# Value sums emptied on ScalarE instead of VectorE, and turned by plain transposes, in a perceiver layer

## The chip, the cores and the metric

The kernel runs on one core of a Trainium2 chip. The metric is the device time of one execution in microseconds (us): the median of several runs. TensorE multiplies matrices and writes to PSUM; VectorE and ScalarE work on rows of PSUM and SBUF; GpSimd works on SBUF alone; SyncE (SP) issues the DMAs. Each engine works through its own queue in order, and the queues wait for each other by semaphores. In the profile PE is TensorE, PEld its weight loads, DVE is VectorE, ACT ScalarE and POOL GpSimd.

## The reference

A layer of three residual blocks on 128 batches of 32 rows of 128 features: cross-attention on a context of 257 rows, causal self-attention, and a mixture of experts. The change lies in the first block alone:

```python
def _L0_xattn_ref(queries, keys, values, mask):   # keys = values = ctx
    ...
    scale = 1.0 / jnp.sqrt(jnp.asarray(E, q.dtype))
    scores = jnp.einsum('blhe,bshe->bhls', q, k)   # 16 heads of 8 features
    A = jax.nn.softmax(scale * scores, axis=-1)
    A = A * mask                                   # 32 x 257
    out = jnp.einsum('bhls,bshd->blhd', A, v)
    out = jnp.transpose(out, (0, 2, 1, 3)).reshape(B, L, -1)
    return out
...
x = x + _L0_xattn_ref(_layernorm(x, axis=-1), ctx_1024, ctx_1024, fside_SxS2_0)
```

## The kernel before, in words

Three stages run one after the other, one for each block of the reference. The first works on 16 tiles of 8 batches. A tile has 16 steps, and 8 steps (4 batches) are a half-tile; there are 32 half-tiles, counted by `m`. A step takes half of a batch's 16 heads: two groups of four heads by 32 query rows, 128 rows of scores by 257 columns of the context each.

The order is written out by hand in a `steps` function for each engine, and the engines run it with lags. In step `s` TensorE issues the `scores` of step `s`, the transposes of the probabilities of step `s - 2` (`turn_probs`), and at some steps more: at the fourth and eighth step of a half-tile the products of probabilities and values of two batches (`weigh_values`, into the PSUM tile `AV`), at the third and the seventh the transposes of context rows into keys (`turn_keys`), at the sixth `turn_out`. VectorE takes the `maxima` of step `s` and moves the turned, masked probabilities of step `s - 2` to SBUF (`keep_probs`). ScalarE does the `exponentials` of step `s` behind these maxima, and copies keys and queries.

The context has 257 rows; 256 go through TensorE and the last is added by itself. `AV` holds, for each batch, 128 rows (four groups of 32 features) by four heads and 32 queries; only where a row's head is the column's head is the value of use. In the fifth step of the next half-tile VectorE evicts `AV` to `O_m` and multiplies by that mask (`keep_sums`). In the sixth TensorE multiplies `O_m` with a 0/1 matrix `gather_d`, which turns it and adds up the four heads' columns of which three are zero (`turn_out`), into the PSUM tile `MISC`; VectorE scales it by the inverse sums of exponentials (`own_outputs`, into `O_n`). GpSimd forms the last context row's share (`last_products`) and adds it (`add_last`). Once per tile VectorE turns `O_n` (`turn_tile`) and GpSimd adds it to the residual `X` (`add_tile`). `MISC` is shared: keys, queries and outputs all go through it, so `turn_keys` waits for `own_outputs` of the half-tile before.

SP's queue is in order too. In the first tile it waits for `o_last`, which `last_products` sets, then loads the last context rows anew and issues the second half of the residual loads, and only behind them the next inputs:

```python
                    sp.wait_ge(o_last, 2 * t + 1)
                    sp.nop(nofuse=True)
                    load_all(sp, t + 1, 0)
                    if fresh:
                        for q in range(HQ // 2, HQ):
                            load_residual(q)
```

Of the kernel before, what the change touches and what calls it, by code (L numbers as in the profile page):

```python
# [9 lines left out]
ALU = mybir.AluOpType  # L10
ACT = mybir.ActivationFunctionType
# [3 lines left out]
B, L, D = 128, 32, 128  # L15
# [14 lines left out]
HSTEPS = STEPS // 2  # L30
DECAY = -0.25
# [3 lines left out]
def perceiver_layer(nc, x, ctx, fmask, Wq, bq, Wk, bk, Wv, bv, Wo, bo, gate_w, w1, b1, w2, b2, ln_g, ln_b, out):  # L35
    with ExitStack() as es:
        def sb(name, shape, dt=F32):
            return es.enter_context(nc.sbuf_tensor(name, shape, dt))
# [8 lines left out]
        gather_d = sb("gather_d", [P, NQ, DK])  # L47
# [56 lines left out]
        with ExitStack() as s1:  # L104
            def sb1(name, shape, dt=F32):
                return s1.enter_context(nc.sbuf_tensor(name, shape, dt))
# [4 lines left out]
            def sem1(name):  # L111
                return s1.enter_context(nc.semaphore(name))
# [4 lines left out]
            last_p = sb1("last_p", [P, HB * NQ])  # L117
            last_x = sb1("last_x", [P, HB * NQ, HQ, DK])
            last_y = sb1("last_y", [P, HB * NQ, 2, DK])
            last_v = sb1("last_v", [P, HB * NQ, DK])  # L120
            last_o = sb1("last_o", [P, HB * NQ, DK])
# [14 lines left out]
            rden = sb1("rden", [P, HB * NQ])  # L136
            Et = sb1("Et", [P, HSTEPS, 2, KT, HQ * L])
# [21 lines left out]
            p_last, v_last, o_last, o_both = sem1("p_last"), sem1("v_last"), sem1("o_last"), sem1("o_both")  # L159
            q_first = sem1("q_first")  # L160
            av_ps = sem1("av_ps")
            rden_set = sem1("rden_set")
# [114 lines left out]
            def _(pool):  # L277
# [32 lines left out]
                def last_products(t, h):  # L310

                    m = 2 * t + h
                    pool.wait_ge(all_in[h], 16 * (t + 1))
                    pool.tensor_tensor(last_x[:, :, :, :],
                                       last_all[:, h, :, :].rearrange("p j (g q d) -> p (j g) q d", g=NQ, q=HQ),
                                       block_of[:, :].unsqueeze(1).unsqueeze(3).to_broadcast([P, HB * NQ, HQ, DK]),
                                       ALU.mult).then_inc(v_last, 1)
                    pool.wait_ge(v_last, 3 * m + 1)
                    pool.tensor_tensor(last_y[:, :, :, :], last_x[:, :, 0:2, :], last_x[:, :, 2:4, :], ALU.add).then_inc(v_last, 1)
                    pool.wait_ge(v_last, 3 * m + 2)  # L320
                    pool.tensor_tensor(last_v[:, :, :], last_y[:, :, 0, :], last_y[:, :, 1, :], ALU.add).then_inc(v_last, 1)
                    pool.wait_ge(v_last, 3 * m + 3)
                    pool.wait_ge(p_last, m + 1)
                    pool.tensor_tensor(last_o[:, :, :], last_v[:, :, :],
                                       last_p[:, :].unsqueeze(2).to_broadcast([P, HB * NQ, DK]), ALU.mult).then_inc(o_last, 1)

                def add_last(t, h):

                    m, n = 2 * t + h, HB * NQ
                    pool.wait_ge(o_n, m + 1)  # L330
                    pool.wait_ge(o_last, m + 1)
                    mine = O_n[:, :, n * h:n * (h + 1)].rearrange("p d u -> p u d")
                    pool.tensor_tensor(mine, mine, last_o[:, :, :], ALU.add).then_inc(o_both, 1)
# [9 lines left out]
                def steps(t, fresh, final):  # L343
                    for h in range(2):
                        if not (final and h == 1):
                            place_queries(*((t, 1) if h == 0 else (t + 1, 0)))
                        if h == 1 and not fresh:
                            add_tile(t - 1)
                        if not final:
                            power(t + 1, h)  # L350
                        if not (fresh and h == 0):
                            last_products(*((t, 0) if h == 1 else (t - 1, 1)))
                            add_last(*((t, 0) if h == 1 else (t - 1, 1)))
# [12 lines left out]
                pool.wait_ge(dve_set, 11)  # L366
                run_tiles(steps, pool)
                last_products(T - 1, 1)
                add_last(T - 1, 1)
# [3 lines left out]
            def _(pe):  # L373
# [82 lines left out]
                def turn_out(t, h, final=False):  # L456
                    m = 2 * t + h
                    pe.wait_ge(o_m, m + 1)
                    if not final:
                        pe.wait_ge(kt_sb, 2 * m + 4)  # L460
                    for j in range(HB):
                        i = pe.matmul(MISC[:, 32 * j:32 * j + 32], O_m[:, j, :], gather_d[:, :, :].rearrange("p g d -> p (g d)"),
                                      start=True, stop=True)
                    i.then_inc(o_ps, 1)
# [43 lines left out]
                pe.wait_ge(dve_set, 11)  # L508
# [21 lines left out]
            def _(act):  # L530
# [35 lines left out]

# [7 lines left out]
                run_tiles(steps, act)  # L574

            @block.vector
            def _(dve):
# [49 lines left out]

                def last_probs(t, h):
                    m = 2 * t + h
                    dve.wait_ge(rden_set, m + 1)  # L630
                    if not (isinstance(t, int) and t == 0 and h == 0):
                        dve.wait_ge(o_last, m)
                    dve.scalar_tensor_tensor(last_p[:, :], E[:, h, :, S - 1], mask_col[:, 0:1],
                                             rden[:, :], ALU.mult, ALU.mult).then_inc(p_last, 1)

                def keep_sums(t, h):

                    m = 2 * t + h
                    dve.wait_ge(av_ps, HB * (m + 1))
                    dve.tensor_tensor(O_m[:, :, :].rearrange("p j (q l) -> p j q l", q=HQ),  # L640
                                      AV[:, :, :].rearrange("p j (q l) -> p j q l", q=HQ),
                                      hh_of[:, :].unsqueeze(1).unsqueeze(3).to_broadcast([P, HB, HQ, L]), ALU.mult).then_inc(o_m, 1)

                def own_outputs(t, h):

                    m = 2 * t + h
                    dve.wait_ge(o_ps, m + 1)
                    dve.wait_ge(rden_set, m + 1)
                    if not (isinstance(t, int) and t == 0):
                        if h == 0:  # L650
                            dve.wait_ge(o_t, t)
# [14 lines left out]
                def steps(t, fresh, final):  # L666
                    for s in range(STEPS):
# [3 lines left out]
                        if s % HSTEPS == 4 and not (fresh and s < HSTEPS):  # L671
                            keep_sums(*((t, 0) if s > HSTEPS else (t - 1, 1)))
# [9 lines left out]
                        if not (fresh and s < HSTEPS):  # L682
                            tt, ss = back(t, s, HSTEPS)
                            hh = ss // HSTEPS
                            if s % HSTEPS == 3:
                                invert(tt, hh)
                            if s % HSTEPS == 4:
# [18 lines left out]
                dve.tensor_reduce(gather_d[:, :, :], ident[:, :].rearrange("p (g q d) -> p g d q", g=NQ, q=HQ), AX.X,  # L706
                                  ALU.add).then_inc(dve_set, 1)
# [39 lines left out]
                dve.wait_ge(dve_set, 11)  # L747
# [3 lines left out]
                invert(T - 1, 1)  # L751
                last_probs(T - 1, 1)
                keep_sums(T - 1, 1)
# [952 lines left out]
```

## Time and profile before

| | us |
|---|---|
| median of 3 runs | 1048.88 (1048.84 to 1049.33) |
| the profiled execution | 1050.45 |
| its span, first to last instruction | 1048.7 |
| TensorE busy in the span | 927.9 (88%) |
| VectorE busy | 840.0 (80%) |
| ScalarE busy | 648.9 (62%) |
| GpSimd busy | 606.9 (58%) |

The first stage ends at about 529 us. A busy share over the whole span is a mean over three stages with different limits, so the rows below are from stretches of one stage. An instruction's duration reaches from its start to its end; the next one of the same engine can start before that, so what one costs in a row of them is the distance of the starts.

### The profile page before, as it was taken

What the parts mean: (1) busy time and instruction counts of PE and PEld (TensorE: products, weight loads), DVE (VectorE), ACT (ScalarE), POOL (GpSimd) and SP (SyncE); (2) the same over time, 40 slices, a digit from 0 to 9 for tenths busy, and PEclk for the clock granted to TensorE, in tenths of its full rate; (3) what the DMA queues carried; (4) which work ended last, traced back from release to release, by engine and by line L of the source; (5) the groups of instructions that cost most, each with busy time, mean ns of one, the idle gap of its engine ahead of it and who ended that gap; (6) DMA issues with size and microseconds to landing.
All of it is one profiled execution on the core that took longest, in us unless ns stands there. A gap on an engine that the chain in (4) does not pass through costs nothing. (4 is left out here: it accounts for less than half of the span.)

```text
span 1048.7 us, 25999 instructions
## 1 busy us (share of the span) xinstructions
PE 927.9 (88%) x7666; PEld 815.4 (78%) x7666; DVE 840.0 (80%) x2152; ACT 648.9 (62%) x2006; POOL 606.9 (58%) x531
## 2 busy tenths in 40 slices
PE   3959999999999999999948888878899888888983
PEld 2848888888888888888848888778788787878872
DVE  5747787878788787878758887886499999999995
ACT  2626566656666566666536666666477777767674
POOL 4335555655555564556344444443477777877786
PEclk9979999999999999999969998999999999999997
DMA  4021212212221212221400000000000000000000
GB/s 119 25 74 56 58 50 65 55 47 60 55 65 43 65 55 52 56 65 54 142 1 1 0 0 0 0 0 1 1 2 10 5 10 5 10 5 6 9 5 16
DMA packets 48676, 35.34 MB, mean 34 GB/s; under 512 B 3660, under 2 KB 48392, under 8 KB 48648
## 3 DMA queue, kind: packets, MB, share of 16 engines
q1 hardware_dynamic: 48648, 35.00, 12.2%
q8 instruction: 14, 0.23, 0.1%
q14 instruction: 14, 0.11, 0.0%
HBM read 32.88 MB, written 2.10 MB: 33 GB/s over the span
## 5 line engine op out<-in xcount | busy, mean ns | idle before, releaser
L551 ACT ACTIVATE E<-SC,neg_max 128x257 f32<-128x257 f32 x512 | 238.4, 471 | 161.2 <-DVE neg_max L613 161.1
L425 PE MATMUL SC<-Kt,Qbd 128*128 128x257 f32 x1024 | 279.6, 396 | 1.0 <-ACT E L551 0.8
L613 DVE TENSOR_REDUCE neg_max<-SC 128x2 f32<-128x514 f32 x256 | 177.0, 691 | 86.6 <-PE SC L425 75.2
L425 PEld LDWEIGHTS SC<-Kt,Qbd 128*128 128x128 f32 x1024 | 176.9, 193 | 31.4 <-issue 14.1
L301 POOL TENSOR_TENSOR Qbd<-Qt,head_scaled 128x2048 f32<-128x2048 f32 (+2 forms) x33 | 145.1, 4398 | 80.0 <-ACT Qt L541 80.0
L621 DVE TENSOR_TENSOR Et<-ETP,mask_T 128x512 f32<-128x512 f32 x256 | 174.0, 680 | 15.0 <-PE ETP L439 14.9
L439 PE MATMUL ETP<-ident,E 128*128 128x128 f32 x1024 | 156.1, 275 | 0.0
L1371 PE MATMUL PO<-W,hid 128*128 128x128 f32 x1024 | 138.2, 278 | 18.8 <-ACT hid L1412 18.7
L1371 PEld LDWEIGHTS PO<-W,hid 128*128 128x128 f32 x1024 | 131.4, 192 | 29.0 <-issue 21.5
L1436 ACT ACTIVATE Y<-Z,zb,zs 128x128 f32<-128x128 f32 x256 | 111.0, 485 | 60.1 <-DVE zb L1591 60.1
L439 PEld LDWEIGHTS ETP<-ident,E 128*128 128x128 f32 x1024 | 125.3, 142 | 20.5 <-issue 0.4
L1360 PE MATMUL PH<-xT,W 128*128 128x256 f32 x512 | 135.1, 387 | 0.5 <-ACT xT L1404 0.5
L1412 ACT ACTIVATE hid<-PH,b1c 128x256 f32<-128x256 f32 x256 | 105.5, 463 | 19.3 <-PE PH L1360 17.8
L551 ACT ACTIVATION_READ_ACCUMULATOR E<-SC,neg_max 128x1 f32 x512 | 101.1, 198 | 0.0
L308 POOL TENSOR_TENSOR xrs<-xvar,neg_half 128x1 f32<-128x1 f32 x32 | 17.6, 549 | 134.8 <-DVE xvar L593 134.8
L1360 PEld LDWEIGHTS PH<-xT,W 128*128 128x128 f32 x512 | 87.8, 192 | 9.7 <-ACT xT L1404 0.7
L1268 POOL TENSOR_TENSOR zr<-zv,neg_half 128x8 f32<-128x8 f32 x32 | 60.0, 1875 | 39.6 <-DVE zv L1577 39.6
L1262 POOL TENSOR_TENSOR XB<-xn,b2r 128x512 f32<-128x512 f32 x64 | 81.4, 1275 | 0.8 <-DVE xn L1487 0.8
L1601 DVE TENSOR_TENSOR U<-Y,gr 128x512 f32<-128x512 f32 x64 | 71.2, 1113 | 5.4 <-POOL acc L1274 2.9
L450 PE MATMUL AV<-Et,V 128*32 128x128 f32 x2048 | 69.4, 276 | 0.3 <-DVE Et L621 0.3
L1120 PE MATMUL PY<-Wo,Oc 128*128 128x128 f32 x256 | 39.1, 316 | 29.5 <-DVE Oc L887 29.5
L450 PEld LDWEIGHTS AV<-Et,V 128*32 128x32 f32 x2048 | 51.9, 109 | 11.4 <-issue 10.7
(161 smaller groups left out, 1579.1 us busy)
## 6 DMA issues: line engine op xcount, KB each, us to landing
V<-in_ctx_dram SPq DMA_DIRECT2D x64, 256.0 KB, 2.9
last_all<-in_ctx_dram SPq DMA_DIRECT2D x32, 256.0 KB, 5.0
xh<-in_x_dram SPq DMA_DIRECT2D x32, 64.0 KB, 3.7
X<-in_x_dram SPq DMA_DIRECT2D x32, 64.0 KB
out_dram<-Xo SPq DMA_DIRECT2D x64, 32.0 KB, 1.5
W<-in_L_ffn_w_dram SPq DMA_DIRECT2D x1, 1024.0 KB
W<-in_L_ffn_w_dram SPq DMA_DIRECT2D x2, 512.0 KB
last_row<-in_ctx_dram SPq DMA_DIRECT2D x32, 2.0 KB
```

The source lines that it names most:

```text
L301: pool.tensor_tensor(Qbd[:, h, j0:j1, :, :], Qt[:, j0:j1, :].unsqueeze(2).to_broadcast([P, j1 - j0, H, L]), head_scaled[:, :, :].unsqueeze ...
L425: i = pe.matmul(SC[s % 2][:, u, 0:S], Qbd[:, h, jj, g:g + HQ, :].rearrange("p q l -> p (q l)"), Kt[:, h, jj, 0:S], start=True, stop=True)
L439: i = pe.transpose(ETP[s % 2][:, c:c + P], E[:, h, u0 + u, k * P:(k + 1) * P], ident[:, :])
L450: i = pe.matmul(AV[32 * g:32 * g + 32, j % HB, :], V[:, j, k, 32 * g:32 * g + 32], Et[:, 2 * (j % HB) + g // 2, g % 2, k, :], start=(j % H ...
L551: i = act.activation(E[:, h, u0 + u, :], SC[s % 2][:, u, 0:S], ACT.Exp, bias=neg_max[:, s % 2, u:u + 1], accum_out=den[:, h, u0 + u:u0 + u ...
L613: dve.tensor_reduce(neg_max[:, s % 2, :], SC[s % 2][:, :, 0:S], AX.X, ALU.max, negate=True).then_inc(max_sb, 1)
L621: dve.tensor_tensor(Et[:, s % HSTEPS, :, :, :].rearrange("p u k c -> p (u k c)"), ETP[s % 2][:, :], mask_T[:, :, :, :].rearrange("p u k c ...
L1262: pool.tensor_tensor(XB[:, 2 * p:2 * p + 2, :, :], xn[:, :, :].unsqueeze(1).to_broadcast([P, 2, 2, D]), b2r[:, 2 * p:2 * p + 2, :].unsquee ...
L1360: i = pe.matmul(PH[x % 2][:, a, :], W1[:, x, a * P:(a + 1) * P], xT[:, :], start=True, stop=True)
L1371: i = pe.matmul(PO[p % 2][:, 2 * (x % 2) + e, :], hid[:, x % 2, a, e * P:(e + 1) * P], W2[:, x, a, :], start=(a == 0), stop=(a == FH - 1))
L1412: i = act.activation(hid[:, x % 2, a, :], PH[x % 2][:, a, :], ACT.Gelu, bias=b1c[:, FH * x + a:FH * x + a + 1])
L1436: i = act.activation(Y[:, p % 2, k, :], Z[:, p, k, :], ACT.Identity, scale=zs[:, p // 2, f:f + 1], bias=zb[:, p // 2, f:f + 1])
```

## The change

`keep_sums` moves from VectorE to ScalarE, as a plain copy without the mask, behind the exponentials of the fifth step of a half-tile (`AV_STEP = 4`). `turn_out` becomes four transposes, so `MISC` gets all four heads' columns. VectorE spreads the inverse sums over four columns of which the own one is kept (`spread_shares`, into `own_p`), and `own_outputs` multiplies all 512 columns by it (into `own_x`). The last row's share is formed the same way by one product of 512 columns on GpSimd, and `fold` adds both and then sums the four columns in two more adds. `last_products` now waits for `p_last` at its start and sets `o_last` with its one product.

```diff
+AV_STEP = 4
...
                     pool.wait_ge(all_in[h], 16 * (t + 1))
+                    pool.wait_ge(p_last, m + 1)
                     pool.tensor_tensor(last_x[:, :, :, :],
                                        last_all[:, h, :, :].rearrange("p j (g q d) -> p (j g) q d", g=NQ, q=HQ),
-                                       block_of[:, :].unsqueeze(1).unsqueeze(3).to_broadcast([P, HB * NQ, HQ, DK]),
-                                       ALU.mult).then_inc(v_last, 1)
...
-                    pool.tensor_tensor(last_o[:, :, :], last_v[:, :, :],
-                                       last_p[:, :].unsqueeze(2).to_broadcast([P, HB * NQ, DK]), ALU.mult).then_inc(o_last, 1)
...
+                                       last_p[:, :, :].unsqueeze(3).to_broadcast([P, HB * NQ, HQ, DK]),
+                                       ALU.mult).then_inc(o_last, 1)
...
+                def fold(t, h):
...
                     pool.wait_ge(o_n, m + 1)
                     pool.wait_ge(o_last, m + 1)
-                    mine = O_n[:, :, n * h:n * (h + 1)].rearrange("p d u -> p u d")
-                    pool.tensor_tensor(mine, mine, last_o[:, :, :], ALU.add).then_inc(o_both, 1)
+                    pool.tensor_tensor(last_x[:, :, :, :], last_x[:, :, :, :], own_x[:, :, :, :], ALU.add).then_inc(o_sum, 1)
+                    pool.wait_ge(o_sum, m + 1)
+                    pool.tensor_tensor(pair_x[:, :, :, :], last_x[:, :, 0:2, :], last_x[:, :, 2:4, :], ALU.add).then_inc(o_pair, 1)
...
+                    pool.tensor_tensor(O_n[:, :, n * h:n * (h + 1)].rearrange("p d u -> p u d"),
+                                       pair_x[:, :, 0, :], pair_x[:, :, 1, :], ALU.add).then_inc(o_both, 1)
...
                     for j in range(HB):
-                        i = pe.matmul(MISC[:, 32 * j:32 * j + 32], O_m[:, j, :], gather_d[:, :, :].rearrange("p g d -> p (g d)"),
-                                      start=True, stop=True)
+                        i = pe.transpose(MISC[:, j * P:(j + 1) * P], O_m[:, j, :], ident[:, :])
...
+                def keep_sums(t, h):
+
+                    m = 2 * t + h
+                    act.wait_ge(av_ps, HB * (m + 1))
+                    if not (isinstance(t, int) and t == 0 and h == 0):
+                        act.wait_ge(o_ps, m)
+                    act.activation(O_m[:, :, :], AV[:, :, :], ACT.Copy).then_inc(o_m, 1)
...
                         exponentials(t, s, first=fresh)
+                        if s % HSTEPS == AV_STEP and not (fresh and s < HSTEPS):
+                            keep_sums(*((t, 0) if s > HSTEPS else (t - 1, 1)))
...
+                def spread_shares(t, h):
+                    m = 2 * t + h
+                    dve.wait_ge(rden_set, m + 1)
+                    dve.tensor_tensor(own_p[:, :, :], rden[:, :].unsqueeze(2).to_broadcast([P, HB * NQ, HQ]),
+                                      block_of[:, :].unsqueeze(1).to_broadcast([P, HB * NQ, HQ]), ALU.mult).then_inc(own_set, 1)
...
-                    dve.tensor_tensor(O_n[:, :, HB * NQ * h:HB * NQ * (h + 1)].rearrange("p d u -> p u d"),
-                                      MISC[:, 0:P].rearrange("p (u d) -> p u d", d=DK),
-                                      rden[:, :].unsqueeze(2).to_broadcast([P, HB * NQ, DK]), ALU.mult).then_inc(o_n, 1)
+                    dve.tensor_tensor(own_x[:, :, :, :], MISC[:, :].rearrange("p (u q d) -> p u q d", q=HQ, d=DK),
+                                      own_p[:, :, :].unsqueeze(3).to_broadcast([P, HB * NQ, HQ, DK]), ALU.mult).then_inc(o_n, 1)
...
-                        if s % HSTEPS == 4 and not (fresh and s < HSTEPS):
-                            keep_sums(*((t, 0) if s > HSTEPS else (t - 1, 1)))
```

On VectorE, in the fifth and sixth step of a half-tile in the loop over tiles (`neg_max` are the maxima, `Et` the kept probabilities), there stands before:

```order
L613 TENSOR_REDUCE neg_max<-SC0 128x2 [waits exp_sb,sc_ps]
L639 ISA
L640 TENSOR_TENSOR O_m<-AV,hh_of 128x512 [waits av_ps]
L584 ISA
L586 BN_AGGR xmv<-xstat 128x2 [waits xstat_sb]
L620 REGISTER_ALU [waits et_ps]
L621 TENSOR_TENSOR Et<-ETP0,mask_T 128x512 [waits av_ps]
L593 TENSOR_SCALAR xvar<-xmv 128x1 [waits xrs_sb,xmean_sb]
L632 REGISTER_ALU [waits rden_set]
L633 SCALAR_TENSOR_TENSOR last_p<-E,mask_col,rden 128x16 [waits o_last]
L610 REGISTER_ALU
L613 TENSOR_REDUCE neg_max<-SC1 128x2 [waits exp_sb,sc_ps]
```

And now, at the same place:

```order
L622 TENSOR_REDUCE neg_max<-SC0 128x2 [waits exp_sb,sc_ps]
L593 ISA
L595 BN_AGGR xmv<-xstat 128x2 [waits xstat_sb]
L629 REGISTER_ALU [waits et_ps]
L630 TENSOR_TENSOR Et<-ETP0,mask_T 128x512 [waits av_ps]
L602 TENSOR_SCALAR xvar<-xmv 128x1 [waits xrs_sb,xmean_sb]
L647 REGISTER_ALU [waits own_set]
L648 SCALAR_TENSOR_TENSOR last_p<-E,mask_col,own_p 128x64 [waits o_sum]
L619 REGISTER_ALU
L622 TENSOR_REDUCE neg_max<-SC1 128x2 [waits exp_sb,sc_ps]
L630 TENSOR_TENSOR Et<-ETP1,mask_T 128x512 [waits av_ps,et_ps]
L658 TENSOR_TENSOR own_x<-MISC,own_p 128x512 [waits o_sum,own_set,o_ps]
```

The eviction `O_m` has left its place between the maxima of the fifth step and the variance `xvar`; the product of the own quarter, `own_x`, stands where the scaled output stood, two rows below this piece of before.

On ScalarE, in the fifth and sixth step of the loop's first half-tile (`E` are the exponentials, two of a step, and `SC0` is the score tile of the even steps), before:

```order
L551 ACTIVATE E,den<-SC0,neg_max 128x257 [waits max_sb]
L551 ACTIVATE E,den<-SC0,neg_max 128x257
L546 REGISTER_ALU
L551 ACTIVATE E,den<-SC1,neg_max 128x257 [waits max_sb]
L551 ACTIVATE E,den<-SC1,neg_max 128x257
L546 REGISTER_ALU
```

And now:

```order
L549 ACTIVATE E,den<-SC0,neg_max 128x257 [waits max_sb]
L549 ACTIVATE E,den<-SC0,neg_max 128x257
L556 ISA
L558 REGISTER_ALU [waits av_ps]
L559 ACTIVATE O_m<-AV 128x512 [waits o_ps]
L544 REGISTER_ALU
L549 ACTIVATE E,den<-SC1,neg_max 128x257 [waits max_sb]
L549 ACTIVATE E,den<-SC1,neg_max 128x257
```

The eviction stands between the exponentials of the two steps, with a wait for the value sums and one for the transposes of the half-tile before.

On TensorE, from the fifth step's score transposes to the seventh step's scores, now (before, the four rows of `O_m` were products with `gather_d` of 32 columns, at the same place):

```order
L438 MATMUL ETP1<-ident,E 128x128 [waits et_sb,exp_sb]
L438 MATMUL ETP1<-ident,E 128x128 x3
L457 ISA
L459 ISA [waits o_m]
L461 MATMUL MISC<-ident,O_m 128x128 [waits kt_sb]
L461 MATMUL MISC<-ident,O_m 128x128 x3
L421 REGISTER_ALU
L424 MATMUL SC0<-Kt,Qbd 128x257 [waits exp_sb]
L424 MATMUL SC0<-Kt,Qbd 128x257
```

The rows and waits around them are as they were: the transposes wait for `o_m`, and the scores of the next step stand behind them.

## Rows read from the trace of the kernel before

**Rows 1.** Busy time of each engine by stretches; PEclk is the granted clock.
```profile
240.00:270.00 30.00, 30.00 (x292) 25.41 (x291) 24.10 (x52) 18.47 (x69) 16.88 (x16) 1.00 0.22 57
```

**Rows 2.** Timeline of TensorE, 240 to 256 us: start, duration, instructions.
```profile
241.50 1.13 PE L425 MATMUL SC<-Kt,Qbd 128*128 128x257 f32 x4
...
242.91 1.03 PE L425 MATMUL SC<-Kt,Qbd 128*128 128x257 f32 x4
243.78 0.60 PE L439 MATMUL ETP<-ident,E 128*128 128x128 f32 x4
244.22 0.98 PE L462 MATMUL MISC<-gather_d,O_m 128*128 128x32 f32 x8
245.03 1.11 PE L425 MATMUL SC<-Kt,Qbd 128*128 128x257 f32 x4
245.98 0.60 PE L439 MATMUL ETP<-ident,E 128*128 128x128 f32 x4
246.42 0.63 PE L394 MATMUL MISC<-ident,V 128*128 128x128 f32 x4
```

**Rows 3.** Timeline of TensorE's weight loads, 243.8 to 246.9 us.
```profile
244.11 0.97 PEld L462 LDWEIGHTS MISC<-gather_d,O_m 128*128 128x128 f32 x8
```

**Rows 4.** Timeline of VectorE, 240 to 272 us; brackets are idle time before.
```profile
242.68 0.69 DVE L613 TENSOR_REDUCE neg_max<-SC 128x2 f32<-128x514 f32 x1 [0.91 <-PE SC L425]
243.29 0.68 DVE L640 TENSOR_TENSOR O_m<-AV,hh_of 128x512 f32<-128x512 f32 x1
...
245.96 0.38 DVE L652 TENSOR_TENSOR O_n<-MISC,rden 128x128 f32<-128x128 f32 x1
...
257.93 0.69 DVE L613 TENSOR_REDUCE neg_max<-SC 128x2 f32<-128x514 f32 x1 [0.91 <-PE SC L425]
...
264.48 0.43 DVE L661 STREAM_TRANSPOSE O_t<-O_n 128x256 f32<-128x256 f32 x1
```

**Rows 5.** Timeline of ScalarE, 240 to 272 us.
```profile
243.40 0.48 ACT L551 ACTIVATE E<-SC,neg_max 128x257 f32<-128x257 f32 x1 [1.49 <-DVE neg_max L613]
...
244.22 0.20 ACT L551 ACTIVATION_READ_ACCUMULATOR E<-SC,neg_max 128x1 f32 x1
...
247.73 0.20 ACT L551 ACTIVATION_READ_ACCUMULATOR E<-SC,neg_max 128x1 f32 x1
247.82 0.59 ACT L533 ACTIVATE Kt<-MISC 128x512 f32<-128x512 f32 x1
```

**Rows 6.** Groups by line and shape, 60 to 470 us: busy, mean ns.
```profile
L314 POOL TENSOR_TENSOR last_x<-last_all,block_of 128x512 f32<-128x512 f32 x26 | 27.0, 1040 | 0.0
...
L319 POOL TENSOR_TENSOR last_y<-last_x 128x256 f32<-128x256 f32 x26 | 19.1, 736 | 2.0
```

**Rows 7.** Timeline of SP's queue, 40 to 96 us.
```profile
51.85 12.57 SPq L198 DMA_DIRECT2D X<-in_x_dram  x16
...
65.95 0.38 SPq L179 DMA_DIRECT2D xh<-in_x_dram  x1
```

**Rows 8.** Timeline of GpSimd, 40 to 96 us.
```profile
48.48 1.03 POOL L314 TENSOR_TENSOR last_x<-last_all,block_of 128x512 f32<-128x512 f32 x1
...
50.95 0.41 POOL L324 TENSOR_TENSOR last_o<-last_v,last_p 128x128 f32<-128x128 f32 x1
```

**Rows 9.** Timeline of VectorE, 40 to 96 us.
```profile
72.50 0.29 DVE L580 BATCH_NORM_STATS2 xstat<-xh 128x6 f32<-128x128 f32 x1 [12.38 <-DMA xh<-in_x_dram]
```

**Rows 10.** Timeline of GpSimd, 516 to 536 us.
```profile
527.10 0.52 POOL L333 TENSOR_TENSOR O_n<-O_n,last_o 128x128 f32<-128x128 f32 x1 [2.10 <-DVE O_n L652]
```

**Rows 11.** Busy time by stretches, behind the long wait and in stage two.
```profile
74.10:80.30 6.20, 6.17 (x23) 5.51 (x24) 3.71 (x8) 2.94 (x11) 3.67 (x6) 0.50 0.04 10
...
680.00:690.00 10.00, 7.95 (x55) 7.71 (x54) 7.44 (x18) 5.63 (x15) 4.50 (x5) 0.83 0.00 0
```

**Rows 12.** Timeline of TensorE, 22 to 31 us.
```profile
27.83 1.06 PE L439 MATMUL ETP<-ident,E 128*128 128x128 f32 x4
...
29.77 0.60 PE L439 MATMUL ETP<-ident,E 128*128 128x128 f32 x4
```

More of the change, by code:

```diff
@@ L46, in perceiver_layer @@
         own_of = sb("own_of", [P, 2, HQ])
-        gather_d = sb("gather_d", [P, NQ, DK])
         hh_of = sb("hh_of", [P, HQ])
@@ L116, in perceiver_layer @@
             last_all = sb1("last_all", [P, 2, HB, D])
-            last_p = sb1("last_p", [P, HB * NQ])
+            last_p = sb1("last_p", [P, HB * NQ, HQ])
             last_x = sb1("last_x", [P, HB * NQ, HQ, DK])
-            last_y = sb1("last_y", [P, HB * NQ, 2, DK])
-            last_v = sb1("last_v", [P, HB * NQ, DK])
-            last_o = sb1("last_o", [P, HB * NQ, DK])
+            own_x = sb1("own_x", [P, HB * NQ, HQ, DK])
+            pair_x = sb1("pair_x", [P, HB * NQ, 2, DK])
             xh = sb1("xh", [P, 2, D])
@@ L136, in perceiver_layer @@
             rden = sb1("rden", [P, HB * NQ])
+            own_p = sb1("own_p", [P, HB * NQ, HQ])
             Et = sb1("Et", [P, HSTEPS, 2, KT, HQ * L])
@@ L158, in perceiver_layer @@
             et_ps, et_sb = sem1("et_ps"), sem1("et_sb")
-            p_last, v_last, o_last, o_both = sem1("p_last"), sem1("v_last"), sem1("o_last"), sem1("o_both")
+            p_last, o_last, o_sum, o_pair, o_both = (sem1(n) for n in ("p_last", "o_last", "o_sum", "o_pair", "o_both"))
             q_first = sem1("q_first")
             av_ps = sem1("av_ps")
-            rden_set = sem1("rden_set")
+            rden_set, own_set = sem1("rden_set"), sem1("own_set")
             o_m, o_ps, o_n, o_t, x1 = (sem1(n) for n in ("o_m", "o_ps", "o_n", "o_t", "x1"))
@@ L313, in last_products @@
                     pool.wait_ge(all_in[h], 16 * (t + 1))
+                    pool.wait_ge(p_last, m + 1)
                     pool.tensor_tensor(last_x[:, :, :, :],
                                        last_all[:, h, :, :].rearrange("p j (g q d) -> p (j g) q d", g=NQ, q=HQ),
-                                       block_of[:, :].unsqueeze(1).unsqueeze(3).to_broadcast([P, HB * NQ, HQ, DK]),
-                                       ALU.mult).then_inc(v_last, 1)
[L318 to L323, printed above, removed]
-                    pool.tensor_tensor(last_o[:, :, :], last_v[:, :, :],
-                                       last_p[:, :].unsqueeze(2).to_broadcast([P, HB * NQ, DK]), ALU.mult).then_inc(o_last, 1)
-                def add_last(t, h):
+                                       last_p[:, :, :].unsqueeze(3).to_broadcast([P, HB * NQ, HQ, DK]),
+                                       ALU.mult).then_inc(o_last, 1)
+                def fold(t, h):
                     m, n = 2 * t + h, HB * NQ
@@ L331, in add_last @@
                     pool.wait_ge(o_last, m + 1)
-                    mine = O_n[:, :, n * h:n * (h + 1)].rearrange("p d u -> p u d")
-                    pool.tensor_tensor(mine, mine, last_o[:, :, :], ALU.add).then_inc(o_both, 1)
+                    pool.tensor_tensor(last_x[:, :, :, :], last_x[:, :, :, :], own_x[:, :, :, :], ALU.add).then_inc(o_sum, 1)
+                    pool.wait_ge(o_sum, m + 1)
+                    pool.tensor_tensor(pair_x[:, :, :, :], last_x[:, :, 0:2, :], last_x[:, :, 2:4, :], ALU.add).then_inc(o_pair, 1)
+                    pool.wait_ge(o_pair, m + 1)
+                    if h == 0 and not (isinstance(t, int) and t == 0):
+                        pool.wait_ge(o_t, t)
+                    pool.tensor_tensor(O_n[:, :, n * h:n * (h + 1)].rearrange("p d u -> p u d"),
+                                       pair_x[:, :, 0, :], pair_x[:, :, 1, :], ALU.add).then_inc(o_both, 1)
                 def add_tile(t):
@@ L352, in steps @@
                             last_products(*((t, 0) if h == 1 else (t - 1, 1)))
-                            add_last(*((t, 0) if h == 1 else (t - 1, 1)))
+                            fold(*((t, 0) if h == 1 else (t - 1, 1)))
                 power(0, 0)
@@ L365, in _ @@
                 pool.memset(Vbd[:, :, :], 0.0).then_inc(pool_set2, 1)
-                pool.wait_ge(dve_set, 11)
+                pool.wait_ge(dve_set, 10)
                 run_tiles(steps, pool)
                 last_products(T - 1, 1)
-                add_last(T - 1, 1)
+                fold(T - 1, 1)
                 add_tile(T - 1)
@@ L507, in _ @@
                 i.then_inc(pe_set, 1)
-                pe.wait_ge(dve_set, 11)
+                pe.wait_ge(dve_set, 10)
                 turn_queries(0, 0, first=True)
@@ L574, in _ @@
                 run_tiles(steps, act)
+                keep_sums(T - 1, 1)
             @block.vector
@@ L626, in invert @@
                     dve.reciprocal(rden[:, :], den[:, h, :]).then_inc(rden_set, 1)
+                def spread_shares(t, h):
[3 more added lines that the diff above has]
+                                      block_of[:, :].unsqueeze(1).to_broadcast([P, HB * NQ, HQ]), ALU.mult).then_inc(own_set, 1)
                 def last_probs(t, h):
                     m = 2 * t + h
-                    dve.wait_ge(rden_set, m + 1)
+                    dve.wait_ge(own_set, m + 1)
                     if not (isinstance(t, int) and t == 0 and h == 0):
[L632 to L642, printed above, removed]
+                        dve.wait_ge(o_sum, m)
+                    dve.scalar_tensor_tensor(last_p[:, :, :], E[:, h, :, S - 1].unsqueeze(2).to_broadcast([P, HB * NQ, HQ]),
+                                             mask_col[:, 0:1], own_p[:, :, :], ALU.mult, ALU.mult).then_inc(p_last, 1)
                 def own_outputs(t, h):
@@ L647, in own_outputs @@
                     dve.wait_ge(o_ps, m + 1)
[L648 to L651, printed above, removed]
-                    dve.tensor_tensor(O_n[:, :, HB * NQ * h:HB * NQ * (h + 1)].rearrange("p d u -> p u d"),
-                                      MISC[:, 0:P].rearrange("p (u d) -> p u d", d=DK),
-                                      rden[:, :].unsqueeze(2).to_broadcast([P, HB * NQ, DK]), ALU.mult).then_inc(o_n, 1)
+                    dve.wait_ge(own_set, m + 1)
+                    if not (isinstance(t, int) and t == 0 and h == 0):
+                        dve.wait_ge(o_sum, m)
+                    dve.tensor_tensor(own_x[:, :, :, :], MISC[:, :].rearrange("p (u q d) -> p u q d", q=HQ, d=DK),
+                                      own_p[:, :, :].unsqueeze(3).to_broadcast([P, HB * NQ, HQ, DK]), ALU.mult).then_inc(o_n, 1)
                 def turn_tile(t):
@@ L686, in steps @@
                                 invert(tt, hh)
+                                spread_shares(tt, hh)
                             if s % HSTEPS == 4:
@@ L705, in _ @@
                                   ALU.mult).then_inc(dve_set, 1)
-                dve.tensor_reduce(gather_d[:, :, :], ident[:, :].rearrange("p (g q d) -> p g d q", g=NQ, q=HQ), AX.X,
-                                  ALU.add).then_inc(dve_set, 1)
                 dve.tensor_reduce(block_of[:, :], ident[:, :].rearrange("p (q l) -> p q l", q=HQ), AX.X,
@@ L746, in _ @@
                 dve.tensor_copy(b1c[:, :], MISC3[:, 0:NE * FH]).then_inc(dve_set3, 1)
-                dve.wait_ge(dve_set, 11)
+                dve.wait_ge(dve_set, 10)
                 run_tiles(steps, dve)
@@ L751, in _ @@
                 invert(T - 1, 1)
+                spread_shares(T - 1, 1)
                 last_probs(T - 1, 1)
-                keep_sums(T - 1, 1)
                 own_outputs(T - 1, 1)
```

## The prediction

> **What bounds the kernel now.** I read the busy table by stretches first. From 240 to 270 us, the middle of the first stage, TensorE is busy 30.00 of 30.00 us at a granted clock of 1.00; VectorE is busy for 24.10, ScalarE for 18.47, GpSimd for 16.88 [rows 1]. So TensorE sets the pace, and what a change is worth there is read from its queue alone. Next, that queue in order of time [rows 2]. A step of scores takes 0.87 us from start to start (242.91 to 243.78), four transposes of probabilities 0.44 (243.78 to 244.22), the four gather products of `turn_out` 0.81 (244.22 to 245.03), and the scores behind them 0.95 (245.03 to 245.98). No row has a wait in brackets. Then, who feeds `turn_out`: VectorE runs the maxima of step 12 (the fifth of its half) at 242.68 for 0.69 us, then at 243.29 the eviction `O_m` for 0.68, so `O_m` is there at 243.97 [rows 4]. TensorE starts loading the first `O_m` weights at 244.11, 0.14 us later [rows 3], just in time for its slot at 244.22. That eviction costs TensorE nothing today, but it has next to no margin. ScalarE does the exponentials of the same step from 243.40, behind the same maxima, and its second accumulator read starts only at 244.22 [rows 5].
>
> **What the change removes on TensorE.** `turn_out` issues 8 weight loads and 8 matmuls per half-tile (each product in two passes); it will issue 4 transposes of 128x128, the form of [rows 2] at 243.78: 0.44 instead of 0.81. The scores behind transposes take 0.87 instead of 0.95. If TensorE never waited, that is 0.37 + 0.08 = 0.45 us per half-tile.
>
> **What it adds on the path.** `keep_sums` now stands on ScalarE behind the exponentials of the step whose maxima used to stand ahead of it on VectorE. Step by step, at the same half-tile: scores start at 241.50 as before; the maxima end at 242.68 + 0.69 = 243.37; the two exponentials start at 243.40 and their last read at 244.22. The next ACTIVATE starts 0.09 us after that read's start, as 247.82 follows 247.73, so the copy starts at 244.31. The trace has no copy from `AV` on ScalarE; the nearest row is the key copy from PSUM of the same 128x512, 0.59 to 0.60 [rows 5]. `O_m` is there at 244.91, not 243.97. With the same 0.14 us the weights start at 245.05, where TensorE was ready at 244.22: a wait of 0.83. Behind the waiting transposes the next scores are queued, and everything else. Transposes 0.44 and 0.02 to fill: 245.51. Scores 0.87: the next transposes of probabilities start at 246.38, against 245.98. That is +0.40 us per half-tile. Nothing later gives it back, since TensorE has no other wait that the delay could fill, and the chain from scores over maxima and exponentials to the copy starts from TensorE itself each time. Bounds: if copy and weights lie only 0.03 apart, as the maxima's end at 243.37 and the exponentials do, it is +0.29; if the scores still take 0.95, +0.48. I take 0.40, as the 0.14 is from this very place of the loop.
>
> There are 32 half-tiles. The first lies ahead of a stall that absorbs it, the second runs at half clock right behind that stall (there the 8 passes cost twice as much, so wait and saving about cancel: +0.1), the last is the tail. 29 x 0.40 = **+11.6 us** (8.4 to 13.9).
>
> **VectorE.** It loses `O_m` (0.60 from 243.29 to the next start); `own_outputs` grows from 128x128, 0.38, to the size of the old eviction, 0.68 [rows 4]; `spread_shares` and the wider `last_p` are 64 columns, under the 0.38 of the 128-column row. They are hidden by the 0.91 idle before the maxima at 242.68. `own_x` starts when the transposes land (0.60 after the first starts, as at 243.78: about 245.7) and ends at 246.4; `turn_keys`, which waits for it, comes to its turn at 246.42 + 0.40 = 246.8, so 0.4 us of cover is left.
>
> **GpSimd.** Two 128-column products go, an add of 512 columns comes. It lies between the 512-column product (1.04) and twice the 256-column add (2 x 0.735 = 1.47) [rows 6]; I take 1.3, nearer the add. `fold` then is 1.3 + 0.74 + 0.52 and gaps of 0.1: from 246.4 to 249.2. In the other half-tile, 15.25 us later (the same maxima at 242.68 and 257.93), VectorE turns the tile at 264.48 [rows 4], now at 264.9; `fold` ends at 264.4. Hidden, with 0.5 left; without the cover it would cost a few tenths in 16 tiles.
>
> **A gain elsewhere.** At 72.50 VectorE had waited 12.38 us for `xh` [rows 9]. That load stands on SP's queue behind 16 residual loads of 12.57 us [rows 7], and these wait for `o_last`. It came with `last_o`, at 50.95 + 0.41 = 51.36; now it comes with the product, which ended at 48.48 + 1.03 = 49.51 [rows 8], and starts 0.6 earlier since the variance on VectorE no longer stands behind `O_m`. So the stall ends 2.4 us sooner: **-2.4** (0, if the loads drain no sooner, to -2.5).
>
> **The tail.** After the last half-tile nothing hides `fold`. Before, one add of 0.52 at 527.10 followed the output product [rows 10]; now 1.3 and 0.74 and their gaps come ahead of it. The shorter transposes and copy give back about what the wider `own_x` takes, and 0.15 more. **+1.9** (1.8 to 2.2).
>
> Sum: 11.6 + 0.1 - 2.4 + 1.9 = **+11.2 us** (7.8 to 16.2). The profiled execution took 1050.45 us, 1.6 above the median of the three runs; set against that median of 1048.88 it gives **1060.1**.
>
> **A rule against the change, and the clock.** A granted clock of 0.50 stood from 74.1 to 80.3 us, after VectorE's long wait had stopped TensorE; from 680 to 690, in the second stage, where TensorE is busy for 7.95 of 10 us, it is 0.83 [rows 11]: some 10 x 0.17 x 2 = 3.4 us at 1.2 GHz, which costs 1.7 us. The change puts a wait of 0.83 between two sets of transposes. Should each such place bring one such stretch, that is 1.7 us a half-tile. Against it: at 27.83 TensorE was still at 1.2 GHz (four transposes took 1.06), and having run them and one step of scores it was at 2.4 GHz by 29.77 (0.60) [rows 12]; and the middle of the first stage is granted 1.00, though ten sets of transposes at 0.44 (eight of probabilities, two of keys) take 4.4 of a half-tile's 15.25 us. The Trainium skill, "TensorE: Matmul & The Clock Gate", section on PE-mode transpose, says that transposes don't count as TensorE being busy in the same way, which speaks for the drop; the rise at 29 us speaks against it, and no row decides it for a wait of this kind.
>
> **Rivals.**
> 1. TensorE doesn't wait: the copy arrives in time, and only the saving is left. 31 x 0.45 = 14.0 off, with -2.4 and +1.9: **1034**, faster. It decides from the point where `O_m` is there 0.37 us sooner than I reckon, at 244.54. For it: the value sums are complete well before, and ScalarE idles 1.49 us ahead of these exponentials [rows 5]. Against it: ScalarE works in order, and the copy is written behind them. Chance 0.05.
> 2. The wait is about half as long (a quicker copy or restart), and saving and wait cancel: about **1049**. Chance 0.04.
> 3. The clock falls too, in half of the half-tiles: 15 x 1.7 = 26 more, **1086**; in all, about 1113. Chance 0.07.
> 4. My forecast, **1060.1**: 0.84.
>
> **How the numbers follow.** Under the forecast, the bounds give 1056.7 to 1065.1; the second stage's half-clock stretches may fall one more or one fewer, 1.7 us either way. 1055 to 1067 leaves out rivals 1 to 3, 0.16, and little else. A measurement of this kernel can tell about 0.2%, 2.1 us, from no change: faster 0.05 (rival 1), same 0.04 (rival 2), slower 0.91.
>
> **What would show it.** Right: before `turn_out`'s first transpose TensorE idles about 0.8 us for ScalarE's `O_m`, some 30 times, 24 us in all; the half-tile grows from 15.25 to about 15.65; the wait for `xh` shrinks to about 10; the add in `fold` takes 1.0 to 1.5. Wrong: no such wait (rival 1), a clock under 1.00 between 90 and 510 us (rival 3), or waits of `turn_keys` for `own_x` and of the tile's turn for `fold`, where I have cover.

## The result, and the profile after

The changed kernel took 1061.55 us (median of four runs, 1061.16 to 1062.21), the kernel before 1049.08 (four runs, 1048.84 to 1049.33). The ratio is 1.0119, with a 95% interval of 1.0102 to 1.0137: slower by 1.2%. The profiled execution took 1062.21 us with a span of 1060.5, which is 11.8 more than the span before. All that follows about the place of these 11.8 us is read from the two profiled executions.

Busy time by stretches of the changed kernel comes first, with the columns of [rows 1]: the middle of the first stage, then nearly all of that stage.

```profile
240.00:270.00 30.00, 28.66 (x277) 23.76 (x276) 23.93 (x51) 18.71 (x69) 16.93 (x14) 1.00 0.22 57
90.00:510.00 420.00, 401.84 (x3834) 334.32 (x3834) 337.65 (x687) 267.66 (x973) 243.08 (x176) 1.00 0.20 55
```

TensorE, which was busy for 30.00 of 30.00 us, now idles 1.34 us of them, and 18.16 of 420; the clock is granted in full all the way. The next view is TensorE's timeline at the place of [rows 2], with the scores behind `turn_out` of the third and of the 31st half-tile around it (these two starts measure the length of a half-tile below).

```profile
90.88 1.03 PE L424 MATMUL SC<-Kt,Qbd 128*128 128x257 f32 x4
...
243.82 1.03 PE L424 MATMUL SC<-Kt,Qbd 128*128 128x257 f32 x4
244.69 0.60 PE L438 MATMUL ETP<-ident,E 128*128 128x128 f32 x4
245.95 0.65 PE L461 MATMUL MISC<-ident,O_m 128*128 128x128 f32 x4 [0.66 <-ACT O_m L559]
246.44 1.03 PE L424 MATMUL SC<-Kt,Qbd 128*128 128x257 f32 x4
247.31 0.60 PE L438 MATMUL ETP<-ident,E 128*128 128x128 f32 x4
247.75 0.60 PE L393 MATMUL MISC<-ident,V 128*128 128x128 f32 x4
...
526.02 1.03 PE L424 MATMUL SC<-Kt,Qbd 128*128 128x257 f32 x4
```

The transposes of line 461 were due 0.44 us after 244.69, at 245.13, and start at 245.95: 0.82 late. (The bracket says 0.66 since it counts from the modelled end of the transposes ahead.) ScalarE's timeline says why:

```profile
244.31 0.48 ACT L549 ACTIVATE E<-SC,neg_max 128x257 f32<-128x257 f32 x1 [1.49 <-DVE neg_max L622]
...
245.13 0.20 ACT L549 ACTIVATION_READ_ACCUMULATOR E<-SC,neg_max 128x1 f32 x1
245.23 0.59 ACT L559 ACTIVATE O_m<-AV 128x512 f32<-128x512 f32 x1
```

The copy starts 0.10 behind the start of the second accumulator read, takes 0.59 and ends at 245.82; TensorE starts 0.13 later. ScalarE stood idle for 1.49 us just ahead of these exponentials, but the copy is queued behind them. The waits from 60 to 470 us, grouped by who waits for whom (total, times, longest):

```profile
PE MISC L461 <- ACT O_m L559: 26.3, 26, 9.6
...
DVE xstat L589 <- DMA xh<-in_x_dram: 9.5, 1, 9.5
```

Of the 26 waits the longest, 9.6, is the one in the long stall for `xh`; the other 25 share 16.7, 0.67 each. Nothing waits for GpSimd's sums here. The rows of that stall, in VectorE's timeline and then in SP's, answer to [rows 9] and [rows 7]:

```profile
70.29 0.29 DVE L589 BATCH_NORM_STATS2 xstat<-xh 128x6 f32<-128x128 f32 x1 [9.51 <-DMA xh<-in_x_dram]
```

```profile
49.17 0.37 SPq L174 DMA_DIRECT2D last_all<-in_ctx_dram  x1
49.59 12.41 SPq L198 DMA_DIRECT2D X<-in_x_dram  x16
...
63.53 0.38 SPq L179 DMA_DIRECT2D xh<-in_x_dram  x1
```

The 16 residual loads begin at 49.59 instead of 51.85, and `xh` comes to its turn at 63.53 instead of 65.95. GpSimd's timeline, in the middle of the stage and at its end:

```profile
247.41 1.27 POOL L325 TENSOR_TENSOR last_x<-last_x,own_x 128x512 f32<-128x512 f32 x1 [0.74 <-DVE own_x L658]
248.76 0.74 POOL L327 TENSOR_TENSOR pair_x<-last_x 128x256 f32<-128x256 f32 x1
249.58 0.46 POOL L331 TENSOR_TENSOR O_n<-pair_x 128x128 f32<-128x128 f32 x1
...
534.60 1.26 POOL L325 TENSOR_TENSOR last_x<-last_x,own_x 128x512 f32<-128x512 f32 x1 [0.92 <-DVE own_x L658]
535.94 0.73 POOL L327 TENSOR_TENSOR pair_x<-last_x 128x256 f32<-128x256 f32 x1
536.75 0.46 POOL L331 TENSOR_TENSOR O_n<-pair_x 128x128 f32<-128x128 f32 x1
```

The new 512-column add takes 1.26 to 1.27 us. In the tail the three adds span 534.60 to 537.21, where one of 0.52 stood [rows 10].

For the ledger two more rows of the kernel before are needed, the scores behind `turn_out` of the same two half-tiles (TensorE's timeline; `x2`, since the stretch that was asked for ends within the group of four):

```profile
93.08 0.68 PE L425 MATMUL SC<-Kt,Qbd 128*128 128x257 f32 x2
...
518.13 0.68 PE L425 MATMUL SC<-Kt,Qbd 128*128 128x257 f32 x2
```

| stretch | before | after | difference |
|---|---|---|---|
| start to the third half-tile's `turn_out` done | 93.08 | 90.88 | -2.2 |
| 28 half-tiles from there | 425.05 | 435.14 | +10.1 |
| to the first statistics of stage two (529.37, 538.96) | 11.24 | 12.94 | +1.7 |
| stages two and three, to the end of the span | 519.3 | 521.5 | +2.2 |
| sum | | | +11.8 |

A half-tile grew from 425.05 / 28 = 15.18 us to 15.54, by 0.36.

### The profile page after: what moved, and what is told of

Same layout as the page of the kernel before. It is cut to its first block and busy times, and to the rows that moved or that the text cites. A ratio compares the mean times of both kernels' runs of the same rounds, so it can differ in the third digit from the quotient of the medians.

```text
span 1060.5 us, 25732 instructions
## 1 busy us (share of the span) xinstructions
PE 917.7 (87%) x7538; PEld 800.4 (75%) x7538; DVE 849.3 (80%) x2151; ACT 664.5 (63%) x2038; POOL 619.3 (58%) x499
## 3 DMA queue, kind: packets, MB, share of 16 engines
q1 hardware_dynamic: 48648, 35.00, 11.8%
## 5 line engine op out<-in xcount | busy, mean ns | idle before, releaser
L424 PE MATMUL SC<-Kt,Qbd 128*128 128x257 f32 x1024 | 276.6, 393 | 1.0 <-ACT E L549 0.8
L1122 PE MATMUL PY<-Wo,Oc 128*128 128x128 f32 x256 | 41.7, 330 | 29.7 <-DVE Oc L889 29.7
L1122 PEld LDWEIGHTS PY<-Wo,Oc 128*128 128x128 f32 x256 | 37.8, 234 | 32.8 <-DVE Oc L889 32.8
```

The lines of the kernel that those rows point to most:

```text
L424: i = pe.matmul(SC[s % 2][:, u, 0:S], Qbd[:, h, jj, g:g + HQ, :].rearrange("p q l -> p (q l)"), Kt[:, h, jj, 0:S], start=True, stop=True)
L1122: i = pe.matmul(PY[:, e * D:(e + 1) * D], Oc[:, a:a + HQ, :, :].rearrange("p a b g -> p (a b g)"), W["o"][:, :], start=(q == 0), stop=(q = ...
```

## The experiments

The theory to test has three parts. The loss comes from where the copy stands in ScalarE's queue, not from ScalarE as such nor from the plain transposes; the transposes by themselves save about half a microsecond per half-tile; and once the wait for `O_m` is gone, `own_x` is next to be late. The rivals are that the plain turn and its wider products cost as much wherever the copy stands, that the copy moved earlier brings the whole saving and no new wait, and that the clock suffers. Each expectation gives its own numbers. Times of experiments are medians of four runs; each ratio is to seven runs of the kernel before on the same chip (1052.38 us for the first four experiments, 1051.34 for the others). The figures for a half-tile are worked out as above, over the same 28.

**The copy one step earlier.**

```diff
-AV_STEP = 4
+AV_STEP = 3
```

> The copy on ScalarE goes one step earlier, behind the exponentials of the fourth step, where ScalarE idles 1.49 us. Theory A (the wait is all in the copy's place behind the fifth step's exponentials): TensorE no longer waits for O_m and keeps its saving of 0.45 us per half-tile; but the key transposes then come to their turn before own_x is ready (own_x starts 3.89 us behind the fifth step's scores and takes 0.69, the keys are due at 4.35 to 4.46) and wait about 0.27. Net against before -0.21 per half-tile, -6 in all, with -2.4 for the earlier loads and +1.9 for the tail: 1042 us. Theory B (the wider outputs or the copy on ScalarE cost by themselves, wherever the copy stands): no change against the changed kernel, 1061. Theory C (the key transposes do not come to wait): 1036.

1042.41 us, ratio 0.9907 (0.9878 to 0.9936). No wait for `O_m` is left, and a half-tile takes 14.93. TensorE's timeline, then VectorE's:

```profile
253.18 0.60 PE L438 MATMUL ETP<-ident,E 128*128 128x128 f32 x4
253.61 0.60 PE L461 MATMUL MISC<-ident,O_m 128*128 128x128 f32 x4
254.05 1.03 PE L424 MATMUL SC<-Kt,Qbd 128*128 128x257 f32 x4
254.92 0.60 PE L438 MATMUL ETP<-ident,E 128*128 128x128 f32 x4
255.63 0.63 PE L393 MATMUL MISC<-ident,V 128*128 128x128 f32 x4
```

```profile
254.20 0.68 DVE L630 TENSOR_TENSOR Et<-ETP,mask_T 128x512 f32<-128x512 f32 x1
254.80 0.68 DVE L658 TENSOR_TENSOR own_x<-MISC,own_p 128x512 f32<-128x512 f32 x1
```

The transposes of line 461 follow those of the probabilities at once (253.18 to 253.61). The key transposes behind them don't: 0.71 here, and 0.61 to 0.62 in every other half-tile, instead of 0.44. `own_x` ends at 255.48, and TensorE goes on 0.15 later. So moving one copy by one step turns a kernel that is 1.2% slower into one that is 0.9% faster, and a second wait, which the first had covered, shows.

**The same, and `own_outputs` ahead of `keep_probs` in the sixth step.**

```diff
-AV_STEP = 4
+AV_STEP = 3
...
+                        if s % HSTEPS == 5 and not (fresh and s < HSTEPS):
+                            own_outputs(*((t, 0) if s > HSTEPS else (t - 1, 1)))
...
-                            if s % HSTEPS == 5:
-                                own_outputs(tt, hh)
```

> As the copy in the fourth step, and on VectorE own_outputs goes ahead of the sixth step's keep_probs. Theory A: own_x starts at 3.34 us behind the scores and is ready at 4.13, ahead of the keys at 4.35; no wait is left, -0.48 per half-tile against before: 1035 us. Theory B: 1061. If the probabilities kept 0.6 us later hold something up in their turn: 1042 or more.

1035.52 us (1033.93 to 1039.19), ratio 0.9841 (0.9811 to 0.9871). Its busy time by stretches, and the place in TensorE's timeline:

```profile
90.00:505.00 415.00, 414.89 (x4029) 350.48 (x4027) 349.64 (x713) 277.84 (x1019) 250.53 (x183) 1.00 0.23 64
```

```profile
250.64 0.60 PE L461 MATMUL MISC<-ident,O_m 128*128 128x128 f32 x4
251.08 1.03 PE L424 MATMUL SC<-Kt,Qbd 128*128 128x257 f32 x4
251.95 0.60 PE L438 MATMUL ETP<-ident,E 128*128 128x128 f32 x4
252.39 0.60 PE L393 MATMUL MISC<-ident,V 128*128 128x128 f32 x4
```

TensorE is again busy for all but 0.11 of 415 us, and each set of transposes here takes 0.44. A half-tile takes 14.66, 0.52 less than before. That is what the plain transposes are worth once nothing waits for them: 0.45 was reckoned, and two places that the prediction's sum left out (below) give most of the rest.

**All of the change, but the copy on VectorE at its old place.**

```diff
-                    act.activation(O_m[:, :, :], AV[:, :, :], ACT.Copy).then_inc(o_m, 1)
+                    dve.tensor_copy(O_m[:, :, :], AV[:, :, :]).then_inc(o_m, 1)
```

> All of the change but the move: the plain copy stays on VectorE at its old place behind the fifth step's maxima. Theory A: O_m is there in time, TensorE does not wait for it, but VectorE comes to own_x 0.6 us later, it ends 5.19 us behind the scores and the key transposes, due at 4.46, wait about 0.85: +0.37 per half-tile against before, 1060 us, with no wait at O_m and one of 0.8 at the keys. Theory B (the move alone is at fault, nothing else waits): 1035 to 1037.

1061.25 us, ratio 1.0093 (1.0063 to 1.0123), and 15.52 per half-tile: as slow as the change. The wait has moved. TensorE's timeline:

```profile
242.86 0.60 PE L438 MATMUL ETP<-ident,E 128*128 128x128 f32 x4
243.30 0.60 PE L461 MATMUL MISC<-ident,O_m 128*128 128x128 f32 x4
243.73 1.03 PE L424 MATMUL SC<-Kt,Qbd 128*128 128x257 f32 x4
244.60 0.60 PE L438 MATMUL ETP<-ident,E 128*128 128x128 f32 x4
245.82 0.66 PE L393 MATMUL MISC<-ident,V 128*128 128x128 f32 x4 [0.61 <-DVE own_x L655]
```

`O_m` is in time, but the key transposes, due at 245.04, start at 245.82. VectorE does the copy of 0.68 in the fifth step, runs without a gap from there, and gets to the wide `own_x` only at 245.08. So VectorE can't carry copy and wide product at these places; what ScalarE was given was work that VectorE had no room for, at a place one step too late.

**The kernel before, with only the copy moved.** The old products with `gather_d` stay; the copy goes without its mask to the place of the change, so the sums over four columns are not those of the reference.

```diff
-                    dve.tensor_tensor(O_m[:, :, :].rearrange("p j (q l) -> p j q l", q=HQ),
-                                      AV[:, :, :].rearrange("p j (q l) -> p j q l", q=HQ),
-                                      hh_of[:, :].unsqueeze(1).unsqueeze(3).to_broadcast([P, HB, HQ, L]), ALU.mult).then_inc(o_m, 1)
...
+                    act.activation(O_m[:, :, :], AV[:, :, :], ACT.Copy).then_inc(o_m, 1)
```

> The kernel before with one part alone: keep_sums on ScalarE as a plain copy behind the fifth step's exponentials, so the mask is left out and the output differs. Theory A: the wait of 0.83 us per half-tile comes in full, and the products with gather_d still take 0.81: +0.80 x 29 = 23 and 1 at the half-clock place, less about 0.6 for the earlier loads: 1072 us. Theory B (the wider outputs cost, not the place): near 1049.

1078.11 us, ratio 1.0249 (1.0221 to 1.0278): 26 slower, more than expected, and 16.07 per half-tile. TensorE's timeline:

```profile
253.28 0.60 PE L439 MATMUL ETP<-ident,E 128*128 128x128 f32 x4
254.54 1.07 PE L462 MATMUL MISC<-gather_d,O_m 128*128 128x32 f32 x8 [0.66 <-ACT O_m L561]
255.45 1.11 PE L425 MATMUL SC<-Kt,Qbd 128*128 128x257 f32 x4
```

The wait is the same, 0.82 past the due 253.72. The products then take 0.91 to the scores, where they took 0.81 without a wait [rows 2]: restarting behind a wait costs 0.10 more, which the expectation lacked. The half-tile times stand together now:

| turn | copy | us per half-tile |
|---|---|---|
| products with `gather_d` | VectorE (before) | 15.18 |
| products with `gather_d` | ScalarE, fifth step | 16.07 |
| plain transposes | ScalarE, fifth step (the change) | 15.54 |
| plain transposes | VectorE, fifth step | 15.52 |
| plain transposes | ScalarE, fourth step | 14.93 |
| plain transposes | ScalarE, fourth step, `own_x` first | 14.66 |

The move alone costs 0.89; the plain turn (with its wider products), with the copy on ScalarE, gives back 0.53.

**The copy one step later,** so that the wait between two sets of transposes is near three times as long: this asks the clock.

```diff
-AV_STEP = 4
+AV_STEP = 5
```

> The changed kernel with the copy one step later, behind the sixth step's exponentials (AV_STEP 5). Theory A: TensorE's wait grows from 0.83 to 2.36 us per half-tile (exponentials 3.42 us behind the fifth step's scores, copy from 4.33 to 4.93, weights at 5.07, due at 2.71); half-tile 17.07 us, 1107 in all, if the granted clock stays at 1.00. Theory B (the place of the copy does not matter): 1061. On the clock: should waits between transposes bring it down, some stretches at 1.2 GHz stand between 90 and 510 us and the time is over 1115; none at a wait of 0.83.

1105.98 us, ratio 1.0528 (1.0503 to 1.0552), 17.05 per half-tile. Busy time by stretches, and one wait in TensorE's timeline:

```profile
90.00:490.00 400.00, 347.44 (x3300) 289.00 (x3299) 292.50 (x596) 231.84 (x842) 210.58 (x153) 1.00 0.19 50
```

```profile
244.88 0.60 PE L438 MATMUL ETP<-ident,E 128*128 128x128 f32 x4
247.68 0.65 PE L461 MATMUL MISC<-ident,O_m 128*128 128x128 f32 x4 [2.20 <-ACT O_m L559]
```

TensorE waits 2.36 us (247.68 less the due 245.32) in each half-tile, and the granted clock is 1.00 from 90 to 490 us.

**The loads wait for the fold.** `last_products` sets `o_last` early in the changed kernel; here SP waits for the end of `fold` instead.

```diff
-                    sp.wait_ge(o_last, 2 * t + 1)
+                    sp.wait_ge(o_both, 2 * t + 1)
```

> The changed kernel, but SP's queue waits for o_both (the end of fold) instead of o_last before the second half of the residual loads. If the gain at the stall of the first tiles comes from the earlier o_last, the residual loads start 3.3 us later and VectorE's wait for xh grows from 9.5 to 12.8 us: 1065 us. If the loads set it by themselves: 1061.5 and a wait of 9.5.

1063.47 us (1063.28 to 1066.04), ratio 1.0111 (1.0094 to 1.0127). Each ratio is to runs of the kernel before of its own session (1051.34 here, 1049.08 for the changed kernel), and by the ratios, 1.0111 and 1.0119, the two can't be told apart: the loss that was expected doesn't show in the times. In the traces it does. SP's timeline and VectorE's:

```profile
52.34 0.37 SPq L174 DMA_DIRECT2D last_all<-in_ctx_dram  x1
52.76 12.43 SPq L198 DMA_DIRECT2D X<-in_x_dram  x16
...
66.72 0.38 SPq L179 DMA_DIRECT2D xh<-in_x_dram  x1
```

```profile
73.41 0.29 DVE L589 BATCH_NORM_STATS2 xstat<-xh 128x6 f32<-128x128 f32 x1 [12.75 <-DMA xh<-in_x_dram]
```

Loads that are released 3.17 us later bring `xh` to its turn 3.19 later, and the statistics start 3.12 later. The first statistics of stage two are still 3.17 later than in the changed kernel (542.13 against 538.96). The stall hangs on what releases SP.

**No late half of the residual loads.** This is the second experiment's kernel with all 32 residual loads issued at the start.

```diff
-                        for q in range(HQ // 2):
+                        for q in range(HQ):
...
-                    if fresh:
-                        for q in range(HQ // 2, HQ):
-                            load_residual(q)
```

> The version with the copy in the fourth step and own_outputs first, and all residual loads issued in one piece at 11 us, where SP's queue is idle until 38, instead of half of them behind o_last. If the wait for xh stands behind those loads alone, it vanishes (10.5 us), and with it about 4.5 us at half clock that follow it (2.2 us): 1023 us. If the loads slow the first tiles instead, no better than 1035.

1024.43 us (1023.21 to 1025.50), ratio 0.9736 (0.9720 to 0.9752). The stretch that held the stall:

```profile
60.00:90.00 30.00, 30.00 (x288) 25.35 (x289) 25.20 (x53) 20.26 (x75) 18.03 (x13) 1.00 0.23 59
```

TensorE is busy all the way and at full clock, where the kernel before waited and then ran at 0.50 [rows 9, 11]. The stall and the half clock behind it were worth 11 us (1035.52 to 1024.43, on two chips; the ratios, 0.9841 and 0.9736, say the same). In the two traces the third half-tile's scores behind `turn_out` start at 77.59 instead of 89.57, 12.0 sooner; 12.7 had been expected. This version beats both kernels: it is 2.6% faster than the kernel before, where the change was 1.2% slower.

## Why the prediction held

The forecast was 1060.1 us (1055 to 1067), the time 1061.55.

**The wait for `O_m`.** Predicted 0.83, measured 0.82, step by step: the copy 0.10 behind the accumulator read (0.09), 0.59 long (0.59 to 0.60), the transposes 0.13 after its end (0.14). The key copy from PSUM was the right row to take for a copy that the trace didn't have. The sum also let the first transpose start together with its weight load, without a reason, though 0.11 lies between the two before [rows 2, 3]; behind the wait both start at 245.95. That it is the place in the queue, the first experiment shows: with the same copy one step up the wait is gone.

**The length of a half-tile.** Predicted +0.40, measured +0.36. At the place itself the loss is 0.43, since the transposes take 0.49 behind the wait (245.95 to 246.44), not 0.46. Two places that the sum left out give 0.05 back: they took 0.464 each before and 0.437 after, in the medians over 22 half-tiles in the middle. They are the transposes of probabilities behind the scores, and the key transposes behind these. That makes +0.37; the last 0.01 was not found. Over 28 half-tiles: 10.1 instead of 11.2.

**The earlier loads.** Predicted -2.4 at the stall, measured 72.50 to 70.29, -2.2. The run with late loads shows that the release is the cause. By the third half-tile's scores the kernel is again 2.2 ahead, although that half-tile loses 0.5 up to there (a wait of 0.83, then 0.49 for 0.81): some 2.7 of gain, where -2.4 and +0.1 were reckoned. The difference is the clock's. TensorE's timeline behind the stall, in the kernel before and then in the changed one:

```profile
79.41 1.49 PE L425 MATMUL SC<-Kt,Qbd 128*128 128x257 f32 x4
80.73 0.60 PE L439 MATMUL ETP<-ident,E 128*128 128x128 f32 x4
```

```profile
77.17 1.03 PE L424 MATMUL SC<-Kt,Qbd 128*128 128x257 f32 x4
78.03 0.60 PE L438 MATMUL ETP<-ident,E 128*128 128x128 f32 x4
```

These scores take 1.32 to the next start before and 0.86 now. The granted clock was 0.50 until 80.3 before [rows 11], and until 77.1 in the changed kernel (the last row of this document). So TensorE, which started again 1.3 sooner (72.86, not 74.13), had its full clock 3.2 sooner. The sum had nothing for this, and no run says why; it is luck that it goes the way of the forecast gain.

**The tail and GpSimd.** Predicted +1.9, measured +1.7 from the 31st half-tile on. The add was bounded by 1.04 and 1.47 and set at 1.3; it takes 1.27. `fold` stays hidden, as nothing waits for it between 60 and 470 us. `own_x` ends at 246.64 + 0.69 = 247.33, 0.42 ahead of the key transposes at 247.75: the cover of 0.4 is there. But the prediction didn't say what that cover was made of. It was the wait itself: when it goes, the first experiment has TensorE late by 0.18 to 0.27 for `own_x`.

**Stages two and three.** Predicted 0, give or take 1.7; measured +2.2, in code that the change doesn't touch. From the first statistics to the end of the span they took 519.3 us before, 521.5 after, and 519.4 to 524.3 in the seven experiments, whose edits don't touch them either. So the allowance was too small for one profiled execution. The traces show what goes with it: summed over these stages, the granted clock stood at 0.50 for 58.5 us before, for 60.7 after, and for 58.6 (519.4 us) to 70.3 (524.3 us) in the experiments, in nearly the same order as the times. What sets these stretches was not tested.

The terms make -2.3 + 11.2 + 0.4 (the third half-tile) + 1.9 = +11.2 predicted, and -2.2 + 10.1 + 1.7 + 2.2 = +11.8 measured. The total is nearer than its parts, and that is luck: half-tiles that cost 1.1 less than reckoned are made up for by later stages that took 2.2 more.

**The rivals.** No wait at all, 1034: it needed `O_m` sooner by 0.37, which the queue's order didn't give; once the order does and `own_x` moves up too, the time is 1035.52. The half wait: not seen. The clock: 1.00 from 90 to 510 us, and also with waits of 2.36. (The half clock that the prediction reads at 27.83 us rests on the durations of [rows 12] alone; the profile's granted clock says 1.00 from 20 to 31 us.) The Trainium skill, "TensorE: Matmul & The Clock Gate", section on PE-mode transpose, says that transposes don't count as TensorE being busy in the same way, by which such a place could have cost clock. No run here showed that it does: both sides of these waits are transposes, and no clock was lost in any half-tile of that stretch.

## What to carry to other kernels

Moving work to the engine with more idle time is judged by where it stands in that engine's queue, not by the idle share: here the change cost 1.2% with the copy at one step and won 0.9% with it one step earlier. A wait on the engine that sets the pace covers others behind it, so cover that is reckoned in its presence has to be reckoned again for the version without it. And a load that stands in an ordered queue behind others is as early as what releases the first of them: the stall in the first tile, taken away, was worth about as much as the whole regression (11 of 12 us).

## What the runs showed that was not expected

Behind a wait TensorE loses more than the wait: four transposes took 0.49 to the next scores instead of 0.44, and the eight matmuls of 32 columns with `gather_d` 0.91 instead of 0.81.

Waits of 2.36 us in every half-tile, between two sets of transposes, left the granted clock at 1.00 for 400 us. The long wait for `xh` did not: in the changed kernel TensorE stood still for 9.58 us before 72.86, and the clock is granted at 0.50 from within that wait until 4.2 us after it:

```profile
66.90:77.10 10.20, 4.24 (x16) 3.77 (x17) 4.82 (x11) 3.17 (x12) 3.75 (x5) 0.50 0.14 37
```
